# An adaLN feed-forward kernel on one core: the weighted gates turned by VectorE in sixteen 32x32 blocks instead of by TensorE in one matmul

## The reference

```
x = x + ffn0(cond0(x))      # cond0: a 64x64 mixing of the 64 channels, its matrix blended from 8 by a small network
x = x + ffn1(cond1(x))      # cond1: a grouped 9-tap convolution along the 1024 columns, plus a row from the condition

ffn(y): base = y @ W_base.T + b_base                                  # 1024 x 1024
        w    = gates of 8 experts from y @ W_gate.T                    # layer 0: softmax less threshold, kept if >= 0, normed
                                                                       # layer 1: top 2, softmax over them
        h    = y @ A.T                                                 # 8 experts x 16 columns = 128
        out  = base + 2 * sum over experts of (h_e * w_e) @ B_e        # (rows x 128) @ (128 x 1024)
```

## Time and profile before

| | |
|---|---|
| time, median of 3 runs | 2189.41 us (2189.12 to 2191.34) |
| the profiled execution's own time | 2188.57 us |
| its span, first to last instruction | 2186.8 us |
| granted TensorE clock, mean | 0.996 |
| PE busy | 2143.8 us (98%) |
| DVE busy | 1356.8 us (62%) |
| POOL busy | 856.8 us (39%) |
| ACT busy | 508.9 us (23%) |
| one step of layer 0 | 16.12 us |
| one step of layer 1 | 17.13 us |

### The profile page before, as it was taken

The page is one execution under the profiler, slowest core; times in us unless marked ns, Lnnn a source line. Parts: engine busy times, 40 slices in busy tenths (PEclk is TensorE's granted clock), DMA queues, the critical chain, the costliest instruction groups (busy, mean ns, idle before and its releaser), DMA issues.

```text
span 2186.8 us, 40976 instructions
## 1 busy us (share of the span) xinstructions
PE 2143.8 (98%) x12684; PEld 2099.0 (96%) x12684; DVE 1356.8 (62%) x3539; ACT 508.9 (23%) x1179; POOL 856.8 (39%) x1052
## 2 busy tenths in 40 slices
PE   4999999999999999999999999999999999999998
PEld 4899999999999999999999999999999999999998
DVE  6777777777777777777555554555555555555554
ACT  3222121121222212222322222222222222222221
POOL 5534444344343443444533333333333333333331
PEclk9999999999999999999999999999999999999999
DMA  5433433333334333343544333344333343333432
GB/s 171 133 106 90 110 100 102 108 90 109 101 100 110 90 107 103 94 111 95 170 132 137 130 118 123 123 131 135 119 121 126 128 136 121 118 128 123 137 126 77
DMA packets 163554, 256.34 MB, mean 117 GB/s; under 512 B 21072, under 2 KB 103376, under 8 KB 163536
## 3 DMA queue, kind: packets, MB, share of 16 engines
q1 hardware_dynamic: 163232, 255.55, 38.0%
q10 hardware_dynamic: 304, 0.56, 0.1%
HBM read 122.01 MB, written 100.73 MB: 102 GB/s over the span
## 4 chain that ended last, share of the span: by engine, by line
PE 95%; DMA 1%; DVE 1%; ACT 1%; issue 1%; POOL 0%; SPq 0%; DVEq 0%; ACTq 0%
PE psB L870 73%; PE psB L896 8%; PE psT L846 3%; PE psT L852 3%; PE psT L850 3%; PE psT L851 3%; PE psT L847 1%; PE psB L883 1%; DMA Xraw<-in_x 0%; DMA shifted<-mixbuf 0%; DMA stage<-in_l0w 0%; POOL Wlo L347 0%; DMA outb<-in_condw 0%; ACT Whi L474 0%; SPq L322 0%
## 5 line engine op out<-in xcount | busy, mean ns | idle before, releaser
L870 PE MATMUL psB<-Whi,Yhi 128*128 128x384 f32 (+2 forms) x3072 | 732.3, 346 | 7.4 <-issue 7.4
L870 PE MATMUL psB<-Wlo,Yhi 128*128 128x384 f32 (+2 forms) x3072 | 714.7, 341 | 0.0
L870 PE MATMUL psB<-Whi,Ylo 128*128 128x384 f32 (+2 forms) x3072 | 710.9, 340 | 0.0
L356 POOL TENSOR_TENSOR Xlo<-Xraw,Xhi 128x256 fp32r<-128x256 f32 x512 | 419.9, 853 | 728.1 <-ACT Xhi L432 728.1
L870 PEld LDWEIGHTS psB<-Wlo,Yhi 128*128 128x128 f32 x3072 | 560.5, 189 | 0.0
L870 PEld LDWEIGHTS psB<-Whi,Ylo 128*128 128x128 f32 x3072 | 559.8, 189 | 0.0
L870 PEld LDWEIGHTS psB<-Whi,Yhi 128*128 128x128 f32 x3072 | 526.6, 190 | 22.2 <-issue 7.8
L385 POOL TENSOR_TENSOR res<-res,bias 128x256 f32<-128x256 f32 x256 | 183.3, 748 | 439.4 <-DMA res<-x_scratch 439.4
L448 ACT CAST Yhi<-Y 128x512 fp32r<-128x512 f32 x256 | 159.3, 622 | 602.1 <-DVE Y L619 342.6
L375 POOL TENSOR_TENSOR res<-Xraw,bias 128x256 f32<-128x256 f32 x256 | 223.1, 906 | 114.8 <-DVE outb L655 114.8
L625 DVE TENSOR_TENSOR Ylo<-Y,Yhi 128x512 fp32r<-128x512 f32 x256 | 210.3, 822 | 47.3 <-ACT Yhi L448 47.3
(11 more groups left out here) (90 smaller groups left out, 1899.3 us busy)
## 6 DMA issues: line engine op xcount, KB each, us to landing
Xraw<-in_x SPq DMA_DIRECT2D x64, 512.0 KB, 3.4
x_scratch<-outb SPq DMA_DIRECT2D x64, 512.0 KB, 2.7
x_block_scratch<-outb SPq DMA_DIRECT2D x512, 64.0 KB, 2.0
Xraw<-x_block_scratch SPq DMA_DIRECT2D x64, 512.0 KB, 4.8
res<-x_scratch SPq DMA_DIRECT2D x64, 512.0 KB, 4.4
out<-outb SPq DMA_DIRECT2D x64, 512.0 KB, 3.0
shifted<-mixbuf SPq DMA_DIRECT2D x128, 224.0 KB, 2.5
row<-row_scratch SPq DMA_DIRECT2D x128, 64.0 KB, 4.4
```

Source lines behind the costliest of these rows:

```text
L356: last = pool.tensor_tensor(Xlo[:, piece], Xraw[:, par, piece], as_f32(Xhi[:, piece]), ALU.subtract)
L870: last = mm(psB[:, 3 * par + b, 0:cols], y, w[:, k, BANK0[b]:BANK0[b] + cols], start=(k == 0 and y is yh and w is Whi), stop=(k == KT - 1 ...
```

## The change

`turn` moves from PE to DVE. There it stands right behind `weigh`, ahead of the chunks of tile n+1, and is sixteen transposes of 32x32 blocks from `hw` into a new SBUF tile `HT`; `high_ht` and `low_ht` read `HT` instead of PSUM. The wait of `weigh` for the earlier turn goes, since both are now on one engine; `turn` waits for `hw`, and for `ht_hi` and `ht_lo` of the tile before; `high_ht` gets a wait for `up_done` of the tile before.

```diff
--- before.py
+++ after.py
@@ -54,7 +54,8 @@
 MIX_AFTER = (0, 1, 2, 3)
 CONV_AFTER = (0, 1, 2, 2)
 MIX_AFTER_FIRST = (1, 3, 4, 5)
-TURN_AFTER, UP_AFTER = (4, 2), (5, 3)
+UP_AFTER = (5, 3)
+SQ = 32
 PIECES = 4
 NC = 4
 CH = H // NC
@@ -107,7 +108,7 @@
         agg = sb("agg", [P, C])
         M = sb("M", [P, 2, P], F32R)
         ag = sb("ag", [P, NAG[0]])
-        hw = sb("hw", [P, P])
+        hw, HT = sb("hw", [P, P]), sb("HT", [P, P])
         HThi, HTlo = sb("HThi", [P, P], F32R), sb("HTlo", [P, P], F32R)
         ident = sb("ident", [P, P])
         iota = sb("iota", [P, E_])
@@ -124,11 +125,6 @@
         psB = ctx.enter_context(nc.psum_tensor("psB", [P, 6, HB], F32))
         psT = ctx.enter_context(nc.psum_tensor("psT", [P, 2, HB], F32))
         psG, psW = psB[:, 0, :], psB[:, 1, :]
-
-        def turned(par):
-
-            return psB[:, 3 * par + 2, BANKN[2]:BANKN[2] + P]
-
 
         h0, h1 = Y[:, 0:P], Y[:, P:2 * P]
         conds = outb[:, 1, 0:condw.shape[1]]
@@ -173,7 +169,7 @@
         base_done, ag_copied = sem("base_done"), sem("ag_copied")
         nmax_ready, exp_ready, gate0 = sem("nmax_ready"), sem("exp_ready"), sem("gate0")
         m8_ready, diff_ready, exp2_ready, gate1 = sem("m8_ready"), sem("diff_ready"), sem("exp2_ready"), sem("gate1")
-        hw_ready, tr_done, ht_hi, ht_lo = sem("hw_ready"), sem("tr_done"), sem("ht_hi"), sem("ht_lo")
+        hw_ready, ht_turned, ht_hi, ht_lo = sem("hw_ready"), sem("tr_done"), sem("ht_hi"), sem("ht_lo")
         wts_ready, up_done = sem("wts_ready"), sem("up_done")
         res_ready, rest_added, o_done = sem("res_ready"), sem("rest_added"), sem("o_done")
 
@@ -555,8 +551,10 @@
 
             def high_ht(j, par):
                 n = 2 * j + par
-                act.wait_ge(tr_done, n + 1)
-                nc.scalar.copy(HThi[:, :], turned(par)).then_inc(ht_hi, 1)
+                act.wait_ge(ht_turned, n + 1)
+                if not (isinstance(n, int) and n == 0):
+                    act.wait_ge(up_done, n)
+                nc.scalar.copy(HThi[:, :], HT[:, :]).then_inc(ht_hi, 1)
 
             run(act, step)
             weigh(STEPS - 1, 1, 1)
@@ -750,22 +748,33 @@
                 (gates0 if layer == 0 else gates1)(j, par, bank[:, ER:ER + E_]).then_inc(wts_ready, 1)
                 dve.wait_ge(wts_ready, n + 1)
                 dve.wait_ge(ag_copied, n + 1)
-                if not (isinstance(n, int) and n == 0):
-                    dve.wait_ge(tr_done, n)
                 nc.vector.tensor_tensor(hw[:, :].rearrange("p (e r) -> p e r", e=E_),
                                         ag[:, 0:ER].rearrange("p (e r) -> p e r", e=E_),
                                         bcast(wts, 2, R_), ALU.mult).then_inc(hw_ready, 1)
 
+            def turn(j, par):
+
+                n = 2 * j + par
+                dve.wait_ge(hw_ready, n + 1)
+                if not (isinstance(n, int) and n == 0):
+                    dve.wait_ge(ht_hi, n)
+                    dve.wait_ge(ht_lo, n)
+                for a in range(0, P, SQ):
+                    for b in range(0, P, SQ):
+                        last = nc.vector.transpose(HT[b:b + SQ, a:a + SQ], hw[a:a + SQ, b:b + SQ])
+                last.then_inc(ht_turned, 1)
+
             def low_ht(j, par):
                 n = 2 * j + par
                 dve.wait_ge(ht_hi, n + 1)
-                nc.vector.tensor_tensor(HTlo[:, :], turned(par), as_f32(HThi[:, :]), ALU.subtract).then_inc(ht_lo, 1)
+                nc.vector.tensor_tensor(HTlo[:, :], HT[:, :], as_f32(HThi[:, :]), ALU.subtract).then_inc(ht_lo, 1)
 
             def step(j, par, lay0, lay, lay1, lay2):
                 n = 2 * j + par
                 last_of_0 = isinstance(j, int) and n == STEPS - 1
                 if lay0 is not None:
                     weigh(*before(j, par), lay0)
+                    turn(*before(j, par))
                 if lay1 == 0:
                     evacuate_y(*after(j, par), 0, range(0, 2))
                     if lay2 == 0:
@@ -813,6 +822,7 @@
 
             run(dve, step)
             weigh(STEPS - 1, 1, 1)
+            turn(STEPS - 1, 1)
             low_ht(STEPS - 1, 1)
             add_rest(STEPS - 1, 1)
             emit(STEPS - 1, 1, 1)
@@ -874,14 +884,6 @@
                 if k == KT - 1:
                     last.then_inc(base_done, 1)
 
-            def turn(j, par):
-
-                n = 2 * j + par
-                pe.wait_ge(hw_ready, n + 1)
-                if isinstance(n, int) and n == 0:
-                    pe.wait_ge(consts, 1)
-                mm(turned(par), hw[:, :], ident[:, :], start=True, stop=True, is_transpose=True).then_inc(tr_done, 1)
-
             def up(j, par, layer):
 
                 n = 2 * j + par
@@ -921,8 +923,6 @@
                 mix_after = MIX_AFTER_FIRST if first else CONV_AFTER if lay1 == 1 else MIX_AFTER
                 for k in range(KT):
                     base(j, par, lay, k)
-                    if k == TURN_AFTER[lay] and lay0 is not None:
-                        turn(*before(j, par))
                     for c in range(NC):
                         if k == mix_after[c] and lay1 is not None:
                             mix(*after(j, par), lay1, c)
@@ -930,7 +930,6 @@
                         up(*before(j, par), lay0)
 
             run(pe, step)
-            turn(STEPS - 1, 1)
             up(STEPS - 1, 1, 1)
```

## The result

| | before | after |
|---|---|---|
| median | 2189.26 us (4 runs) | 2425.58 us (4 runs, 2424.46 to 2425.91) |
| span of the profiled execution | 2186.8 us | 2422.7 us |
| granted TensorE clock, mean | 0.996 | 0.971 |
| one step of layer 0 | 16.12 us | 18.09 or 19.65 us |
| one step of layer 1 | 17.13 us | 17.84 and 18.00 by turns |

The account below looks back on a forecast made before the run. PE bounds the kernel, 98% busy and never waiting in a steady step. Layer 0's 155 us, layer 1's 46, 2.5 at the change of layers and 3 at the end sum to 207 on 2188.6: 2396 us, range 2325 to 2510.

Parts of the forecast that it names:

- The price of the blocks: On DVE between hw and chunk 0: each 32x32 transpose starts 0.22 us after the one before, sixteen take 3.5 us.
- T: Time that the sixteen transposes take on DVE in one step: 3.5 us, range 3.4 to 4.6.
- Layer 0's stall: PE starts chunk 2 at 7.52 us instead of 5.52; with late start, less the turn, a step grows 2.0 us.
- The POOL term: Layer 0: POOL's residual ends later and lengthens one or two more gate instructions on DVE, 0.5 us a step.
- emit 0.7 us late: Layer 0: DVE loses its slack, so emit comes 0.7 us late and POOL's residual ends about 2.5 us into the next step.
- PE waits 2 us: Layer 0: PE stands idle 2.0 us ahead of chunk 2 in every step, waiting for DVE's chunk 0.
- case without POOL's term at a pitch of 0.21: Layer 0 without the 0.5 us a step, blocks 0.21 us apart: 2345 us; chance 0.2 for no more POOL trouble.
- Layer 1: PE's chunk 2 stalls 0.74 us; a step grows T - 2.77, about 0.7 us, times 63 steps: 46 us.
- The odd steps: Steps 63 and 64 at the change of layers add some 2.5 us, the last tile's uncovered turn about 3.
- Overlap: Rival: neighbouring blocks on DVE overlap, 0.10 us apart, so PE hardly waits: 2188 us, no change; chance 0.08.
- Blocks waiting for POOL: Rival: layer 1's transposes wait for POOL's residual, up to 2.8 us more in 63 steps, 2570 us; chance 0.10.
- Dearer blocks: Rival: each transpose costs more, 2438 us at 0.24 a block, 2545 at L736's price; chance of 2480 or more 0.12.

Follow-up runs that it names:

- the run behind two chunks: Against the changed kernel, the same sixteen blocks moved behind chunks 0 and 1 in both layers, layer 0's `up` one piece later: 2262.7 us, ratio 1.033 to the kernel before.

## Why the prediction was right, step by step

**The price of the blocks: right.** The pitch was taken as 0.22 us and is 0.217, T 3.5 and 3.48. Its parts were 0.19 for the instruction and 0.02 between two, and the rest a choice between bounds; they are 0.203 and 0.014. That neighbours on other partitions don't overlap, read off one pair, is shown by the runs that keep to the same partitions (0.096) and that swap the loops (0.217). (The prediction counts all sixteen as held. The first starts on partition 0, as the product before it does, and waits for that product in any case; the other fifteen change partitions.) The estimate of a pitch of 0.10 with overlap was right too, and so was its time of 2188.

**Layer 0's stall: right.** A growth of T - 1.51 = 2.0 us was forecast; the short steps grew by 1.97, and with eight blocks (T about 1.73) by 0.23. PE's idle time ahead of chunk 2 is 1.80 us where 2.0 stood in the forecast.

**The POOL term: wrong here.** I had added 0.5 us a step, 31 us in all, since DVE would reach emit 0.7 us late and POOL's residual would then run into the gates. In the changed kernel hw starts at 2.75 us as before and L708 takes 0.43 us as before; that the gate instructions keep their lengths was one of the forecast's own signs of being wrong. Emit starts at 627.50 in the short step, as soon as up is done, and the residual behind it ends 1.81 us into the next step (628.93 + 3.48 - 630.60), where it ended at 1.80 before:

```profile
628.93 3.48 POOL L371 TENSOR_TENSOR res<-Xraw,bias 128x256 f32<-128x256 f32 x4 [1.63 <-DVE outb L653]
```

So the step of the forecast that failed here is "emit 0.7 us late". In that step `low_ht` took 0.28 us and the split behind it 0.69; in the long one 0.74 and 0.89, but there PE was later still, and DVE waited 0.70 us for up. The mechanism exists, and gave 0.7 us a step where the gates are on the chain (the run behind two chunks), but not here.

**The clock: missed.** The step that failed is "PE waits 2 us", priced as 2 us. PE's idle stretch also made the granted clock fall in 33 of 60 steps, 51 us. It stood in no part of the forecast; the run with 16 matmuls of filler shows it. The missing 51 us and the 31 us of POOL that did not come about partly cancel in layer 0 (155 forecast, 179 measured with the first two steps), so that the forecast's total came 30 us from the measured one is in part luck. (In the prediction's case without POOL's term at a pitch of 0.21, 2345 should be 2347; nothing hangs on it.)

**Layer 1: right.** T - 2.77 = 0.7 us a step, 46 us in all; measured 0.78 and 49.

**The odd steps.** 5.5 us were allowed for the change of layers and the end; they came to 8, and the first two steps, for which nothing was allowed, to 10. In the first two PE waits 3.71 and 5.58 us for chunk 2, and the granted clock is 0.50 from 65.78 to 69.19 and from 86.26 to 93.09, where the kernel before had no such stretch. PE works for 8.9 us of those, which at 1.55 us for 3.41 is an estimate of 4 us of the 10.

**The rivals.** Overlap fell with the pitch. Blocks waiting for POOL fell with layer 1's timeline: sixteen take 3.45 us there (1714.78 to 1718.23) while POOL's residual runs beside them (1714.86 to 1717.68), the same as in layer 0, and the longest of all 2048 takes 0.208 us. Dearer blocks fell with 203 ns.

## What to carry to other kernels

Work moved from the bounding engine to one that is 62% busy costs nothing only where that engine is idle: in layer 1 the same sixteen blocks cost 0.78 us a step in one place and gained 0.11 in another, and in layer 0 there was no free place for all of them, since DVE had some 3.5 us of idle time in a step in all (1.73, 1.16 and 0.65, the last of it waiting for ACT amid the gates), for 3.5 us of work. Before inserting work, measure from the timeline the room between the last thing ahead of it and the first wait behind it on the bounding engine, and follow the ring that leads back to the next step. Where TensorE is made to wait, the wait can cost more than its length (here 1.97 us a step and another 1.55 in 33 of 60), so look at the granted clock as well as at the idle time.

## What the runs showed of the hardware that was not expected

- An idle stretch of 1.8 us on TensorE in a step of 18 was followed by 3.41 us at a granted clock of 0.50, in 33 of 60 steps (in 27 none came); filling the stretch with matmuls that nothing reads removed all of them and made the kernel 50 us faster.
- Sixteen transposes of 32x32 float32 take 3.48 us when neighbours read or write different partitions and 1.53 us when they don't; which of the two changes makes no difference (2425.4 and 2425.6 us).
- One transpose instruction takes 203 ns over 32x32 and 312 ns over 128x128 in its 32x32 blocks.
